# A graph-layer kernel for 49 node blocks: the loop over pairs of blocks written out, and its waits given constant values

## The reference

```
transformed = einsum('ni,rio->rno', x, weight)      # 16 matrices of 256 x 256
msg = transformed[edge_type, src] * edge_weight
out = layernorm(x + segment_sum(msg, dst), axis=-1)
```

## Time and profile before

| | us |
|---|---|
| time, median of 3 runs | 2264.51 (2263.26 to 2265.77) |
| span of the profiled execution | 2979.1 |
| PE busy in it | 2249.5 |
| DVE busy | 1566.2 |
| ACT busy | 961.1 |
| POOL busy | 1808.1 |
| mean granted clock of TensorE | 0.770 of full |

### The profile page before, as it was taken

How to read it: one execution, slowest core, us unless ns; L and a number is a source line. 1 busy time by engine, 2 the same in 40 slices (tenths; PEclk the granted TensorE clock), 3 DMA queues, 4 the chain that set the end, 5 groups by cost and what they waited for, 6 DMA issues and landing times.

```text
span 2979.1 us, 46134 instructions
## 1 busy us (share of the span) xinstructions
PE 2249.5 (76%) x13835; PEld 2071.0 (70%) x13835; DVE 1566.2 (53%) x4583; ACT 961.1 (32%) x2224; POOL 1808.1 (61%) x1667
## 2 busy tenths in 40 slices
PE   5877776877787877777778777777786677777777
PEld 4766676767776767676767767766776677766667
DVE  5645455555555555454554556554554455555545
ACT  3333233333323333232332323332333233333322
POOL 6656556666566556556566666665665656565653
PEclk9778777777777777777776778877877778687868
DMA  4322222223222222222222222222222222222222
GB/s 137 88 75 81 77 73 85 78 82 91 70 82 82 71 82 77 78 71 84 69 81 81 74 84 79 82 82 79 75 77 76 85 71 85 71 84 74 82 78 49
DMA packets 106952, 237.04 MB, mean 80 GB/s; under 512 B 30580, under 2 KB 54176, under 8 KB 106926
## 3 DMA queue, kind: packets, MB, share of 16 engines
q0 software_dynamic: 79056, 215.91, 25.1%
q1 hardware_dynamic: 27870, 20.81, 2.4%
HBM read 230.13 MB, written 6.62 MB: 79 GB/s over the span
## 4 chain that ended last, share of the span: by engine, by line
PE 51%; issue 25%; DVE 9%; another core or an unknown queue 7%; ACT 3%; POOL 2%; DMA 1%; DVEq 1%; ACTq 0%; POOLq 0%; SPq 0%
PE ps_a L829 32%; PE ps_z L799 18%; DVE lo L636 4%; DVE onehot L632 2%; ACT hi L729 2%; POOL rows L450 2%; DVE a_lo L606 1%; DMA rows<-in_x,idx 1%; PE ps_m L782 0%; DVEq L331 0%; ACTq L331 0%; ACT a_hi L703 0%; DVE key_in L564 0%; DVE hits L571 0%
## 5 line engine op out<-in xcount | busy, mean ns | idle before, releaser
L450 POOL DMA_INDIRECT rows<-in_x,idx x1646 | 1805.0, 1097 | 1140.7 <-issue 458.3
L829 PE MATMUL ps_a<-onehot,hi 128*128 128x192 f32 (+4 forms) x4410 | 1210.9, 317 | 317.3 <-issue 203.0
L829 PE MATMUL ps_a<-onehot,lo 128*128 128x192 f32 (+4 forms) x4410 | 1218.9, 318 | 181.8 <-issue 179.3
L636 DVE SCALAR_TENSOR_TENSOR lo<-rows,meta,hi 128x256 fp32r<-128x256 f32 x1715 | 816.6, 476 | 976.9 <-ACT hi L729 835.0
L829 PEld LDWEIGHTS ps_a<-onehot,hi 128*128 128x128 f32 x4410 | 914.5, 224 | 396.6 <-issue 255.1
L829 PEld LDWEIGHTS ps_a<-onehot,lo 128*128 128x128 f32 x4410 | 920.7, 226 | 212.1 <-issue 211.6
L729 ACT ACTIVATE hi<-rows,meta 128x256 fp32r<-128x256 f32 x1715 | 735.3, 502 | 193.6 <-DMA rows<-in_x,idx 145.8
L703 ACT ACTIVATE a_hi<-ps_a 128x512 fp32r<-128x512 f32 x392 | 212.8, 595 | 1459.7 <-PE ps_a L829 778.4
L632 DVE TENSOR_SCALAR onehot<-col_iota,key 128x256 fp32r<-128x256 f32 (+4 forms) x1715 | 596.2, 348 | 15.9 <-PE ps_a L829 11.2
L799 PE MATMUL ps_z<-w_hi,a_hi 128*128 128x256 f32 x1568 | 544.4, 347 | 73.9 <-issue 60.4
L799 PE MATMUL ps_z<-w_lo,a_hi 128*128 128x256 f32 x1568 | 504.6, 322 | 69.4 <-issue 68.3
(11 more groups left out here) (56 smaller groups left out, 214.1 us busy)
## 6 DMA issues: line engine op xcount, KB each, us to landing
rows<-in_x,idx POOLq DMA_INDIRECT x1646
xr<-in_x SPq DMA_DIRECT2D x48, 128.0 KB
out<-z_out SPq DMA_DIRECT2D x48, 128.0 KB
w_raw<-in_L_gnn_weight SPq DMA_DIRECT2D x16, 256.0 KB
raw<-in_src SPq DMA_DIRECT2D x48, 17.5 KB
raw<-in_dst SPq DMA_DIRECT2D x48, 17.5 KB
raw<-in_edge_type SPq DMA_DIRECT2D x48, 17.5 KB
raw<-in_edge_weight SPq DMA_DIRECT2D x48, 17.5 KB
```

What stands on the lines that cost most here:

```text
L450: pool.indirect_dma_start(rows[:, rows_slot(b, t), :], None, x, bass.IndirectOffsetOnAxis(ap=idx[:, b[1] % 2, t:t + 1], axis=0), bounds_ch ...
L636: dve.scalar_tensor_tensor(out=lo[:, slot, :], in0=rows[:, rows_slot(b, t), :], scalar=meta[:, b[1] % 2, 3, t:t + 1], in1=hi[:, slot, :].b ...
L829: ins = pe.matmul(ps_a[:, g % OPEN, h, (begin - g * GN) * R:(stop - g * GN) * R], part[:, slot, h * P:(h + 1) * P], onehot[:, slot, (begin ...
```

## The change

The loop is gone. All 49 blocks, and the two programs that end them, are written out on every engine, and a block is a plain number b. A target of a semaphore is then a constant. SP's loop is written out as well. The `sem_inc(ticks, 1)` of these programs are taken out. On GpSimd the value of the late tiles' count is now read once, for tile 33 (n == 0), and both `If`s look at that one register; what `confirm` waits for is still a register's value.

```diff
-        def at(b, per, more):
-
-            u, k = b
-            return k * per + more if u is None else u * (2 * per) + (k * per + more)
-
         def wait(eng, s, b, per, more):
 
-            if b[0] is None and at(b, per, more) <= 0:
-                return
-            eng.wait_ge(s, at(b, per, more))
+            if b * per + more > 0:
+                eng.wait_ge(s, b * per + more)
 
         def blocks(eng, one):
-            one((None, 0), True, False, False)
-            one((None, 1), True, True, False)
-            one((None, 2), True, True, True)
-            with eng.Fori(1, (NB - 1) // 2) as u:
-                one((u, 1), True, True, True)
-                one((u, 2), True, True, True)
-            one((None, NB), False, True, True)
-            one((None, NB + 1), False, False, True)
+            for k in range(NB + 2):
+                one(k, k < NB, 1 <= k <= NB, 2 <= k)
...
-            with sp.Fori(1, NB - 3) as b:
+            for b in range(1, NB - 3):
                 raw_left(b + 2)
-                sp.sem_inc(ticks, 1)
-                load_edges(sp.value_load(first_i[0:1, bass.ds(b + 2, 1)], min_val=0, max_val=E - CE), edges)
+                load_edges(sp.value_load(first_i[0:1, b + 2:b + 3], min_val=0, max_val=E - CE), edges)
 
                 sp.wait_ge(rows_normalised, b)
-                sp.sem_inc(ticks, 1)
-                sp.dma_start(out[bass.ds(b * SB - SB, SB), :], z_out[:, :]).then_inc(rows_out, 16)
-                sp.dma_start(xr[:, :], x[bass.ds(b * SB, SB), :]).then_inc(own_rows_in, 16)
+                sp.dma_start(out[(b - 1) * SB:b * SB, :], z_out[:, :]).then_inc(rows_out, 16)
+                sp.dma_start(xr[:, :], x[b * SB:b * SB + SB, :]).then_inc(own_rows_in, 16)
...
                     if t % BATCH == 0:
 
                         wait(pool, tile_parts_made, b, 2 * CT, 2 * (t + BATCH - ROWS))
-                        pool.sem_inc(ticks, 1)
-                    if t == CONFIRM and not (b[0] is None and b[1] == 0):
+                    if t == CONFIRM and b > 0:
                         confirm()
...
                         if n == 0:
 
                             wait(pool, optional_hits_ready, b, 1, 0)
-                            pool.sem_inc(ticks, 1)
-                        edges = pool.value_load(late_hits[0:1, b[1] % 2, n:n + 1], min_val=0, max_val=P)
+                            edges = pool.value_load(late_hits[0:1, b % 2, n:n + 1], min_val=0, max_val=P)
                         with pool.If(edges > 0):
                             gather(b, t)
                             pool.reg_add(gathered[n], gathered[n], 16)
...
-                base = block_base[:, b[1]:b[1] + 1] if b[0] is None else block_base[:, bass.ds(b[0] * 2 + b[1], 1)]
+                base = block_base[:, b:b + 1]
```

More of the change, by code:

```diff
@@ L450, in gather @@
                 pool.indirect_dma_start(rows[:, rows_slot(b, t), :], None, x,
-                                        bass.IndirectOffsetOnAxis(ap=idx[:, b[1] % 2, t:t + 1], axis=0),
+                                        bass.IndirectOffsetOnAxis(ap=idx[:, b % 2, t:t + 1], axis=0),
                                         bounds_check=last_row, oob_is_err=False).then_inc(rows_in[t], 16)
@@ L469, in gather_block @@
                         wait(pool, tile_parts_made, b, 2 * CT, 2 * (t + BATCH - ROWS))
-                        pool.sem_inc(ticks, 1)
-                    if t == CONFIRM and not (b[0] is None and b[1] == 0):
+                    if t == CONFIRM and b > 0:
                         confirm()
-                    if b[0] is None and b[1] == 0:
+                    if b == 0:
                         if t == SEEK_GATHER:
@@ L548, in keys @@
             def keys(b):
-                k = b[1] % 2
+                k = b % 2
                 wait(dve, edges_copied, b, 1, 1)
@@ L577, in convert_hits @@
                 wait(dve, optional_hits_summed, b, 1, 0)
-                dve.tensor_copy(late_hits[0:1, b[1] % 2, :], ps_f[0:1, HITS_AT:HITS_AT + len(OPTIONAL)]).then_inc(
+                dve.tensor_copy(late_hits[0:1, b % 2, :], ps_f[0:1, HITS_AT:HITS_AT + len(OPTIONAL)]).then_inc(
                     optional_hits_ready, 1)
@@ L585, in normalise @@
                 wait(dve, own_rows_in, b, 16, -16)
-                dve.tensor_tensor(z[:, :], xr[:, :], ps_z[:, b[1] % 2, 0:F], ALU.add).then_inc(residual_added, 1)
+                dve.tensor_tensor(z[:, :], xr[:, :], ps_z[:, b % 2, 0:F], ALU.add).then_inc(residual_added, 1)
                 wait(dve, residual_added, b, 1, -1)
@@ L589, in normalise @@
                 wait(dve, variance_steps, b, 2, -3)
-                dve.sem_inc(ticks, 1)
                 dve.bn_aggr(z_mv[:, :], z_stat[:, :]).then_inc(variance_steps, 1)
@@ L605, in lower_part @@
                     at_g = slice(g * GN, (g + 1) * GN)
-                    dve.tensor_tensor(a_lo[:, b[1] % 2, h, :, at_g],
+                    dve.tensor_tensor(a_lo[:, b % 2, h, :, at_g],
                                       ps_a[:, g % OPEN, h, :].rearrange("p (n r) -> p r n", r=R),
-                                      a_hi[:, b[1] % 2, h, :, at_g].bitcast(F32), ALU.subtract).then_inc(
+                                      a_hi[:, b % 2, h, :, at_g].bitcast(F32), ALU.subtract).then_inc(
                                           a_lower_made, 1)
@@ L644, in tile_block @@
                         if products and t == due - CT:
-                            lower_part((b[0], b[1] - 1), g)
+                            lower_part(b - 1, g)
                     if rows_ and t == NORM_AT:
@@ L653, in fast_vector @@
             dve.memset(eps_col[:, :], EPS).then_inc(columns_made, 1)
-            split_edges((None, 0))
+            split_edges(0)
             dve.wait_ge(window_bases_made, len(runs([first for first, _ in WIN])) + 1)
@@ L658, in fast_vector @@
             dve.wait_ge(constants_made, 6)
-            keys((None, 0))
+            keys(0)
             seek_samples()
@@ L677, in prepare @@
         def prepare(b):
-            return PREPARE_0 if b[0] is None and b[1] == 0 else PREPARE
+            return PREPARE_0 if b == 0 else PREPARE
         def next_edges(step, b):
-            step((b[0], b[1] + 1))
+            step(b + 1)
         def fast_scalar(act):
             def copy_edges(b):
-                k = b[1] % 2
+                k = b % 2
                 wait(act, edges_turned, b, 1, 1)
@@ L702, in evacuate @@
                 for h in range(KH):
-                    act.activation(a_hi[:, b[1] % 2, h, :, g * GN:(g + 1) * GN],
+                    act.activation(a_hi[:, b % 2, h, :, g * GN:(g + 1) * GN],
                                    ps_a[:, g % OPEN, h, :].rearrange("p (n r) -> p r n", r=R),
@@ L729, in tile_block @@
                         act.activation(hi[:, slot, :], rows[:, rows_slot(b, t), :], ACT.Copy,
-                                       scale=meta[:, b[1] % 2, 3, t:t + 1]).then_inc(upper_made, 1)
+                                       scale=meta[:, b % 2, 3, t:t + 1]).then_inc(upper_made, 1)
                     for g in range(GROUPS):
@@ L735, in tile_block @@
                         if products and t == due - CT:
-                            evacuate((b[0], b[1] - 1), g)
+                            evacuate(b - 1, g)
                     if rows_ and t == NORM_AT:
-                        if b[0] is None and b[1] == 2:
+                        if b == 2:
                             act.wait_ge(columns_made, 2)
@@ L743, in tile_block @@
                             deviation_made, 1)
-            copy_edges((None, 0))
+            copy_edges(0)
             blocks(act, tile_block)
@@ L778, in turn_edges @@
                 wait(pe, edges_copied, b, 1, 0)
-                pe.sem_inc(ticks, 1)
                 for a in range(4):
@@ L788, in product @@
                 if n == 0:
-                    if b[0] is None and b[1] == 1:
+                    if b == 1:
                         pe.wait_ge(w_lower_made, R)
@@ L798, in product @@
                 for m, (a_part, w_part) in enumerate(terms):
-                    ins = pe.matmul(ps_z[:, (b[1] + 1) % 2, 0:F], a_part[:, (b[1] + 1) % 2, h, r, :],
+                    ins = pe.matmul(ps_z[:, (b + 1) % 2, 0:F], a_part[:, (b + 1) % 2, h, r, :],
                                     w_part[:, r, h, :], start=n == 0 and m == 0,
@@ L841, in fast_tensor @@
             pe.wait_ge(constants_made, 4)
-            turn_edges((None, 0))
+            turn_edges(0)
             seek_count()
```

8 lines of the change are left out of this document (4 added, 4 removed).

## The result

The changed kernel takes 2308.16 us in the median of 4 runs (2305.2 to 2311.13), the kernel before, on the same chip, 2263.89 us: ratio 1.0199, 95% interval 1.0184 to 1.0215. It is 44 us slower; 33 had been forecast.

A forecast was written before the change was run, and what follows sets the result against it. The prediction took GpSimd's gathers as the bound: 0 for register instructions, loop ends, the dropped reading and fetch, plus 32.6 us for 25 added gathers, on 2264.5, gave 2297 us (chance 0.73). Own range 2280 to 2305; 8 in 10, 2250 to 2312.

The forecast's parts named there:

- The floor: Least time POOL allows: 1646 gathers at 1.305 us plus start and end, 2185 us, 79.5 below the measured time.
- Why the profile of before was 714.6 us longer: Profiled span 2979.1 us against a median of 2264.51 us: the excess was taken as the cost of recording.
- the changed kernel's span, 2917 us: Profiled span from 2979.1 us: 95 us less recorded waiting with fewer records, plus 32.6 us for added gathers.
- Twenty-five more gathers: On POOL, tile 34 gathered wherever tile 33 is: 1671 gathers, 32.6 to 35.2 us more; 32.6 taken.
- Register instructions and loop ends: On DVE, PE, ACT and POOL, removing them gains 0, hidden behind POOL's gathers; at most 79.5 us.
- Instruction fetch and written-out programs: Fetching the straight blocks, about two q8 packets per block for PE, costs 0.
- Rival A: Engines behind POOL set the pace, so added gathers fit into waits: not slower, 2241 us; chance 0.16.
- B: Instruction fetching now stalls POOL, 10 packets at 3.8 us, 38 us: 2335 us; chance 0.06.
- C: Late tiles misread: both counts still decide, 1646 gathers remain and the time stays, 2262 us; chance 0.05.
- The sign given for B: In the changed profile, 1671 gathers with a step longer than 1.31 us without waits would mean B.

The follow-up runs named there:

- undisturbed profile: Kernel before plus 600 register moves in SP's loop body, which never appeared in the trace, making it a repeat of the kernel before; 2265.04 us, 1.0004.
- one reading: Kernel before, loop kept, with the late tiles' count read once, for tile 33, for both Ifs; 2295.68 us, 1.0143 of the kernel before.
- two readings: Changed kernel, written out, but with both late tiles' counts read again, so 1646 gathers; 2275.40 us, 1.0052 of the kernel before.
- TensorE alone: Kernel before with only TensorE's blocks written out, 1646 gathers; 2271.14 us, 1.0036 of the kernel before.
- the other three: Kernel before with the blocks of VectorE, ScalarE and GpSimd written out, TensorE's and SP's loops kept; 2266.70 us, 1.0016 of the kernel before.

## Why the prediction came out as it did

**GpSimd as the bound: right.** The changed kernel's trace shows gathers back to back from the first to the last, and so does the undisturbed one of before. The floor was a sound tool: 2185 us forecast without any wait. The undisturbed profile gives the true excess, 1720.6 - 1646 x 1.00 = 75 us of longer gathers and no waiting; the prediction had 79.5 for both together. Of the 75, 23.6 lie beside the CAST; nearly all the rest lies in gathers during which VectorE builds a one-hot matrix, for the 350 gathers that meet neither are 2 us over in all.

**Why the profile of before was 714.6 us longer: wrong.** The prediction, and the section ahead of it, blamed the profiler's recording. The repeat with the same 46134 records has a span of 2261.4 us, and timed runs carry a span 1.7 to 1.9 us below their time. The disturbed execution is a condition that came back on two other chips, in every run of theirs. The forecast of the changed kernel's span, 2917 us, rested on that error (2309.4). The decision to set aside the shares of that span was still the right one, and the argument that held was another: the gather's pace was free of the disturbance, and multiplied by its count it gave the time of the runs.

**Twenty-five more gathers: right in number and price.** 1671; 1.32 us each measured alone, in the range of 1.305 to 1.41. That the plain step of 1.305 was the price has some luck in it: it holds where the CASTs fall as before (23.6 us beside them, and 23.7 with one reading). Where gathers were taken away or added in more blocks the CASTs moved, and a gather was worth 0.66 and 1.13 us.

**Register instructions and loop ends cost nothing: right.** TensorE written out, with its 2047 register instructions gone, got no faster, and the loop kernel's gathers never wait for longer than 0.7 us. But taking VectorE's out was not neutral: in the kernels with VectorE written out only 1 block of 49 has a CAST that costs its gathers under 0.1 us, in the four with 1646 or 1671 gathers and its loop kept 15 to 19.

**Instruction fetch and written-out programs at 0: wrong.** This is the term that was missed, 12.8 us, and with it the forecast of 33 would have been 45. The ledger of the undisturbed profile shows where it sits. From it to the changed kernel POOL's busy time grows by 1760.6 - 1720.6 = 40.0 us, its idle time by 512.3 - 505.9 = 6.4, and the time after the last gather's end from 30.8 to 32.1; together 47.6 of the 48.0 us between the spans. Of the 40.0, 25 x 1.00 are the new gathers; 15 are gathers made longer. The kernel with two readings, with 1646 gathers, shows the same without them:

```profile
L434 POOL DMA_INDIRECT rows<-in_x,idx x1646 | 1732.9, 1053 | 505.1 <-issue 420.7 <-DVE lo L617 49.1 <-DVE onehot L613 30.8
```

1732.9 - 1720.6 = 12.3 us more busy, and not one wait more. Of the 12.3, 9.0 lie in the two gathers beside the CAST; between the two kernels with 1671 gathers it is 11.1 of 13.4. So most of the missed term goes with VectorE's instruction meeting the gathers in a dearer place, at one point of each block. The prediction had no such term: it looked at VectorE only as the engine that frees row buffers, and at fetching only as a stall of POOL.

I had read from two straight blocks, 53.7 and 54.5 us long under the disturbance, that fetching costs nothing. They could not show a quarter of a microsecond a block. But that fetches lengthen the gathers beside them, the theory of the experiments, is not borne out either. Away from the CAST, gathers during which an instruction packet was moved are 37 ns over in the mean and the others 34 in the changed kernel, 44 and 32 in the one with two readings: with some 220 such gathers that is 1 to 3 us in all. Beside the CAST, where gathers are long, those with a packet are longer too (19 of 148 in the changed kernel, 0.61 against 0.19 us over), but a long gather also meets a packet more easily, so this tells little. What moves the CAST, VectorE's shorter program, a fetch, or TensorE's, is open; TensorE alone added 3.0 us beside the CAST, the other three 4.6.

The Trainium skill, "Runtime: NRT & Kernel Launch", section "Instruction fetch mechanics", says that fetching in sequence is mostly hidden, that a taken branch to code which is no longer held stalls, and that kernels prefer full unrolling partly for that. The traces agree with the stall where it can be seen: SP's straight body, fetched anew, stood 2.6 us in the median after each branch, in the disturbed condition. The loops of the kernel before stayed with their engines (q8 moved 12 packets in all) and had no such stall to lose, and here writing out costs 12.8 us, against the preference.

**Rival A (other engines set the pace): wrong as a whole, with a true corner.** Added gathers were paid in full. But gathers taken away give back only half. The traces put that down not to a row buffer that comes late but to longer gathers beside VectorE's CAST.

**Rivals B and C: no.** POOL has no stall over 0.3 us between gathers, and 1671 gathers were made. The sign given for B, a step over 1.31 us without waits, did come: from the first gather's start to the last's it is (2276.35 - 6.0) / 1670 = 1.36 us. But it is 1.35 us in the undisturbed profile of the kernel before too, so the sign could not tell B from the forecast.

## What to carry to other kernels

Find the engine whose work, at its own undisturbed pace and multiplied by its count, gives the measured time; then count what a change adds there before weighing what it takes off elsewhere. A rewrite meant for form can carry a second edit in an indentation: here one moved line cost 33 of 44 us. A loop whose program stays with its engine is not for free to write out, even where the register instructions saved are in the thousands: when an engine without waits is the bound, look for what makes its instructions longer, and note where the other engines' instructions fall on them. A change that costs the bound nothing by count can still move them.

## What was not expected of the hardware

- VectorE's CAST of 35 x 384 numbers, 0.34 us by itself, lengthens two gathers by some 0.8 us together or by nothing, depending on where in a gather it starts; a few gathers beside it took 1.6 us more and longer.
- The same program took 2264 us on some chips and 2967 to 3007 us on two others, in all runs there. In that disturbed condition SP's reading of a value, 427 to 470 ns in the undisturbed profile, was recorded with 2 to 716 ns, TensorE stood idle for "issue", and 520 semaphore increments took SP 67 to 68 us, longer than a block, so that the kernel became 19% slower. Whether the changed kernel, with 6,400 fewer records, would be the faster one there was not tried.
- A gather's bounds check costs 53 to 56 ns of 1002 (medians, on the chips in the disturbed condition).
- The granted clock averaged 0.90 with GpSimd as the bound, against 0.77 in the disturbed profile.
